# A two-layer propagation kernel: the index stages cut into pieces and run inside the sweeps beside them

## What is computed

```python
n, c, h, w = feature.shape
center = jnp.einsum('nchw,oc->nohw', feature, w_center)
step = jax.nn.relu(jnp.einsum('nchw,oc->nohw', feature, w_step))
prob = jax.nn.sigmoid(jnp.einsum('nchw,oc->nohw', feature, w_prob))
offset = jnp.transpose(center * step, (0, 2, 3, 1)) * STRIDE
th = jnp.minimum(jnp.round(gh[None] + offset[..., 0]), h - 1)
tw = jnp.minimum(jnp.round(gw[None] + offset[..., 1]), w - 1)
tgt = jnp.mod((th * w + tw).reshape(n, h * w).astype(jnp.int32), h * w)
sample = jax.vmap(lambda idx: grid_flat.at[idx].set(grid_flat))(tgt).reshape(n, h, w, 2)
...
sampled = _grid_sample_bilinear(feature, ngrid)
proped = sampled * prob + feature * (1.0 - prob)
return feature * prob + proped * (1.0 - prob)
```

## Time and profile before

| | us |
|---|---|
| median of 3 runs | 10036.8 (10035.82 to 10036.99) |
| the profiled execution | 10041.73 |
| its span | 10039.4 |
| busy: DVE, PE, POOL, ACT | 5791.8, 5688.7, 3805.1, 3314.3 |

### The profile page before, as it was taken

One profiled execution on the slowest core, in us unless ns is written; L12 is line 12 of the kernel. 1 busy time (PEld: TensorE's weight loads), 2 busy tenths in 40 slices (PEclk: granted clock), 3 DMA queues, 4 the chain that ended last, 5 costly groups with the idle time before them and its releaser, 6 DMA issues. The chain is left out here.

```text
span 10039.4 us, 85605 instructions
## 1 busy us (share of the span) xinstructions
PE 5688.7 (57%) x23732; PEld 2719.6 (27%) x23732; DVE 5791.8 (58%) x10809; ACT 3314.3 (33%) x6426; POOL 3805.1 (38%) x9006
## 2 busy tenths in 40 slices
PE   6841078311899988999700221888880011288888
PEld 2320033100444444444300110333330001133333
DVE  3347143571444434444389895666667989566666
ACT  5640066200444544445400000555450000054544
POOL 4530545204445544455400002666650000366665
PEclk8976589765889988899855665888895556588888
DMA  6851268513678876788710003666662000366665
GB/s 218 296 207 46 48 240 298 173 39 63 224 263 297 297 264 226 268 295 299 258 23 0 0 10 69 204 214 217 211 205 64 0 0 10 87 209 212 219 207 193
DMA packets 399395, 1675.31 MB, mean 167 GB/s; under 512 B 112501, under 2 KB 135772, under 8 KB 331621
## 3 DMA queue, kind: packets, MB, share of 16 engines
q1 hardware_dynamic: 203068, 908.43, 28.8%
q10 hardware_dynamic: 131400, 685.12, 16.8%
q0 software_dynamic: 64480, 76.57, 4.1%
HBM read 952.23 MB, written 727.72 MB: 167 GB/s over the span
## 5 line engine op out<-in xcount | busy, mean ns | idle before, releaser
L678 DVE TENSOR_TENSOR ps<-ps,arena 128x400 f32<-128x400 f32 x1600 | 929.9, 581 | 2088.6 <-PE ps L464 1161.7
L437 POOL DMA_INDIRECT arena<-table,gidx x1600 | 1616.5, 1010 | 954.6 <-issue 466.6
L457 PE MATMUL ps<-arena,minus 128*128 128x400 f32 x3200 | 1670.1, 606 | 396.0 <-DVE arena L680 260.2
L388 POOL TENSOR_TENSOR arena<-arena 128x32 f32<-128x32 f32 (+8 forms) x3450 | 808.3, 277 | 1876.2 <-issue 1066.1
L600 ACT ACTIVATE arena<-ps 128x400 f32<-128x400 f32 x1600 | 792.3, 495 | 2096.3 <-PE ps L451 1193.2
L487 PE MATMUL ps<-arena,w_conv 128*10 128x512 f32 (+1 forms) x2800 | 1205.9, 559 | 293.5 <-DMA arena<-x 283.7
L1173 POOL DMA_INDIRECT arena<-table,arena x160 | 151.9, 949 | 3137.4 <-DVEq L1208 2325.3
L606 ACT ACTIVATE arena<-iota,gcol 128x400 f32<-128x400 f32 x800 | 495.0, 619 | 2395.0 <-PEq L1208 2395.0
L540 ACT ACTIVATE arena<-ps 10x512 f32<-10x512 f32 (+1 forms) x1400 | 745.9, 540 | 1356.2 <-PE ps L487 1340.2
L500 PE MATMUL ps<-ident,arena 128*128 128x128 f32 x5000 | 844.8, 314 | 385.1 <-ACT arena L554 199.6
L1110 PE MATMUL ps<-ident,arena 128*1 128x128 f32 x4 | 1.5, 373 | 1731.3 <-DVE arena L856 1731.3
(11 more groups left out here) (195 smaller groups left out, 5357.3 us busy)
## 6 DMA issues: line engine op xcount, KB each, us to landing
arena<-x SPq DMA_DIRECT2D x200, 1600.0 KB
arena<-table SPq DMA_DIRECT2D x200, 1600.0 KB
table<-arena ACTq DMA_DIRECT2D x400, 512.0 KB, 2.7
y<-arena ACTq DMA_DIRECT2D x100, 1600.0 KB
arena<-y SPq DMA_DIRECT2D x100, 1600.0 KB
out<-arena ACTq DMA_DIRECT2D x100, 1600.0 KB
table<-arena ACTq DMA_DIRECT2D x200, 576.0 KB, 8.2
arena<-table,gidx POOLq DMA_INDIRECT x1600
```

The source lines that it names most:

```text
L388: last = E.tensor_tensor(tmp[:, :, at:at + size], cols[:, :, y + to:end + to:step], cols[:, :, y:end:step], ALU.subtract)
L437: pool.indirect_dma_start(got[:, m % DEPTH, e * C:(e + 1) * C], None, rows, bass.IndirectOffsetOnAxis(ap=gidx[:, 2 * m + e:2 * m + e + 1], ...
L457: nc.tensor.matmul(ps[:, 4 + r % 2, 0:W], minus[:, :], tile(t)[:, at], start=True, stop=False)
L678: V.tensor_tensor(d, d, g, ALU.mult).then_inc(s_mix, 1)
```

## The change

Every index stage runs inside a sweep: index 0 in sweep 1, index 1 in sweep 2, index 2 in sweep 3, index 3 in sweep 4. Sweeps 0 and 5 stay alone. The stage's engine functions are generators, and a sweep takes one piece of them per row (`next(work)`), on DVE, PE and ACT, and per tile or per group of four rows on POOL. A row of a sweep is called a slot here (8 a tile, 400 a sweep and some 16 behind). In sweep 1 DVE takes only 0.42 pieces a slot. What a loop with a runtime count holds is one piece: while it runs, DVE (and PE in the far loop) do nothing for the sweep.

```diff
-        sweep(0, None, 0)
-        alone_with(0)
-        sweep(1, None, 1)
-        alone_with(1)
-        sweep(2, 0, 2)
-        sweep(3, 1, 3)
-        alone_with(2)
-        sweep(4, 2, None)
-        alone_with(3)
-        sweep(5, 3, None)
+        sweep(0, None, 0, None)
+        sweep(1, None, 1, 0, pace=0.42, spell=99)
+        sweep(2, 0, 2, 1, spell=11)
+        sweep(3, 1, 3, 2, spell=3)
+        sweep(4, 2, None, 3)
+        sweep(5, 3, None, None)
...
+                def piece(ins, name=None):
+                    note(ins, name)
+                    yield
+                    dve.wait_ge(s_v, n[0])
...
+                compare(0)
+                for i in range(SIDE * SIDE):
+                    dve.wait_ge(s_v, loop0 + 2 * i + 1)
+                    if i + 1 < SIDE * SIDE:
+                        compare(i + 1)
+                    else:
+                        dve.wait_ge(s_v, n[0])
+                    note(V.tensor_tensor(near, near, hit[i % 2], ALU.max))
+                    yield
```

The index stage has its own memory (the first 22440 words of the arena) and PSUM banks 0 and 1. What the sweeps have left for themselves is smaller:

```diff
+            FR = 4 if tabling else 3
+            RR = 3 if listed else 2
+            GB = 2 if listed else 1
+            CB = 1 if mixing else 2
+            WB = 1 if mixing else 2
```

FR are tile buffers (were 4), RR buffers of half a tile of table rows (were two of a whole tile), GB and CB the PSUM banks of gate and products (were 2), WB the scratch of `blend_columns` (was 2). Products come in 8 chunks of 400 pixels instead of 7 of up to 512, and are stored in four pairs through two small buffers; a tile's three table stores go through two buffers instead of six:

```diff
                     def evacuate_conv(t, c):
-                        h = 0 if r < HALVES[0][1] else 1
-                        if r == a and t:
-                            act.wait_ge(s_cst[h], n * 16)
+                        count, nth = n * len(CHUNKS) + c, n * PAIRS + c // 2
+                        if c % 2 == 0 and nth >= 2:
+                            act.wait_ge(s_cst[nth % 2], nth // 2 * 16)
...
                     def evacuate(t, g):
-                        if g == a and t >= 2:
-                            act.wait_ge(s_tst[n % 2][q], n // 2 * 16)
+                        if g == a and nth >= 2:
+                            act.wait_ge(s_tst[nth % 2], nth // 2 * 16)
```

Rows that are blended go in batches of up to four, so that tiles 0 to 7 have two batches, the second of which waits on ACT for DVE's first. The far loop uses two PSUM banks: each of its 16 steps hands over four pieces of 400 columns instead of one of 1600. The index stage's DMAs were issued by SP and are now issued by ACT. Who blends a tile's columns is fixed when the program is made:

```diff
+            def owned(t):
+                if u_idx is None and not mixing:
+                    return "pool" if t % 2 else "dve"
+                now = (t + behind) * BROWS + 3
+                return "dve" if "moved" in born and now <= born["moved"] + BROWS * spell else "pool"
...
+                    if tabling:
+                        for t in range(TILES):
+                            if owner[t] == "pool":
+                                blend_columns(pool, nc.gpsimd, t)
+                            clock[0] = (t + behind + 2) * BROWS + 2
+                            next(work, None)
```

More of the change, by code:

```diff
@@ L93, with batches @@
 GROUPS = len(TURNED) * TILES + len(LATE)
-WEIGHED = [int(bool(INNER[t]) or t in LATE or t + 1 in LATE or t + 1 in EARLY) for t in range(TILES)]
-BLENDED = [int(bool(INNER[t]) or t in EARLY) for t in range(TILES)]
+def batches(t):
+    left, done = list(INNER[t]), []
+    while left:
+        closed = []
+        for y in left:
+            group, todo = {y}, [y]
+            while todo:
+                a = todo.pop()
+                for b in left:
+                    if FIX[b] == a and b not in group:
+                        group.add(b)
+                        todo.append(b)
+            closed.append(sorted(group))
+        best = min(closed, key=len)
+        if done and len(done[-1]) + len(best) <= NEARBY:
+            done[-1] += best
+        else:
+            assert len(best) <= NEARBY
+            done.append(list(best))
+        left = [y for y in left if y not in best]
+    carried = t in LATE or t + 1 in LATE or t + 1 in EARLY or t in EARLY
+    return done or ([[]] if carried else [])
+BATCHES = [batches(t) for t in range(TILES)]
+WEIGHED = [len(BATCHES[t]) if INNER[t] or t in LATE or t + 1 in LATE or t + 1 in EARLY else 0 for t in range(TILES)]
+BLENDED = [len(BATCHES[t]) if INNER[t] or t in EARLY else 0 for t in range(TILES)]
 def turned_before(u, t):
@@ new lines, in turn @@
+                    def turn(t, g):
+                        count, (j0, size) = turned_before(u_tab, t) + g, TURNED[g]
+                        if g == 0:
+                            blended(pe, t)
+                            if BLENDED[t]:
+                                pe.wait_ge(s_hb, counted(BLENDED, u_tab, t + 1))
+                        if count - u_tab * GROUPS >= 2:
+                            pe.wait_ge(s_tevac, count - 1)
+                        pixels = tile(t).rearrange("p (q k) -> p k q", k=COLS)
+                        for j in range(size):
+                            last = nc.tensor.transpose(ps[:, 2 + count % 2, j * PX:(j + 1) * PX], pixels[:, j0 + j, :], ident[:, :])
+                        last.then_inc(s_xpose, 1)
@@ new lines, in _ @@
+                    clock = [0]
+                    work = tensor(pe, clock)
+                    for t in range(ROUNDS):
+                        for r in range(BROWS):
+                            clock[0] = t * BROWS + r
+                            if mixing and here(t):
+                                row(t, r)
+                            elif r < PAIRS and tabling and here(t - behind):
+                                conv(t - behind, 2 * r)
+                            if r < PAIRS and tabling and here(t - behind):
+                                conv(t - behind, 2 * r + 1)
+                            if tabling and here(t - 2):
+                                for g in turns_at(r):
+                                    turn(t - 2, g)
+                            if r == BROWS - 1 and tabling and here(t - 2) and t - 2 in LATE:
+                                turn_late(t - 2)
+                            next(work, None)
@@ L1222, in _ @@
+                    clock[0] = 10 ** 9
+                    for _ in work:
                         pass
```

1537 lines of the change are left out of this document (775 added, 762 removed).

## The result

The changed kernel takes 9964.31 us (median of 8 runs, 9962.4 to 10010.59), the kernel before 10036.9 (8 runs). The ratio is 0.9929, with a 95% interval of 0.9916 to 0.9941: 0.7% faster, where 5.5% was forecast. The profiled execution took 9972.77 with a span of 9971.2.

What follows compares the result with a forecast made beforehand. PE idles in index stages (3618 us) and DVE bounds an ideal overlap; 19.6 + 858 + 1067 + 1850 + 2150 + 2209 + 1327 = 9481 us of span, said as 9480, 5.5% faster, range 8,800 to 9,880.

Steps and rivals of the forecast that it cites:

- DVE sets the pace of sweep 3: Sweep 3 with index 2: 3.9 us a slot set by DVE, 2150 us in sum for 2511 before.
- the store wait: Sweeps 0 to 3: ACT's products wait for a queued small store; 4.6 us a tile in sweep 0, 200 in sweep 2.
- The moved loops' hole: Sweep 2 behind tile 9: POOL's loops of 226 us delay tile 10's blend, while DVE and PE stand; 214 us.
- A far round: One round of the index stages' far loop, run inside a sweep: 82 us.
- The wait of ACT's third pair: Sweep 0: third product pair waits for the first pair's store, queued behind a table store; 4.5 us late a tile.
- Rival A: The store waits cost nothing, as small stores land early; about 8,870 us, chance 22 in 100.
- DVE's blends: Sweep 2, tiles whose columns DVE blends: the sum of 1850 us has no term for them.
- Index pieces in a PE-bound sweep: Sweep 2: DVE has room for most pieces, 30 us for the rest; sweep 1 with index 0 sums to 1067.
- Sweep 4: Sweep 4 with index 3: 310 slots at 5.15 us plus other terms, 2209 us for 2487.5 before.
- Rival B: POOL is shut out of memory while DVE runs index work; about 10,090 us, slower than before, chance 8 in 100.
- Rival C: PE's clock drops where DVE sets the pace, near 0.5 in sweep 3; about 9,840 us, chance 12 in 100.
- Half-tile loads "at nothing": Half-tile row loads cost nothing, as SP waits for buffers anyway; bounded by 1 us a tile, 50 a sweep.

Runs made afterwards that it cites:

- experiment 1: The changed kernel with four product buffers instead of two: 9037.02 us, ratio 0.900; on a further chip 8774.69 us.
- experiment 2: The changed kernel with POOL's moved loops one tile later in its program: 9680.77 us, ratio 0.9649.
- experiment 8: The changed kernel with four product buffers, POOL's loops one tile later and six table buffers in sweep 0: 8490.25 us, ratio 0.8441.
- experiments 1 and 4: The second: the changed kernel with four product buffers, POOL's loops one tile later and DVE blending all columns of sweeps 1 and 2: 9043.88 us.
- experiments 3 and 4: The first: the changed kernel with DVE blending all columns of sweeps 1 and 2: 9953.4 us, ratio 0.9922.

## Why the prediction was wrong

**Right.** Sweeps 3 and 4 gain most, and sweep 2 gains nothing from its overlap (though it was to come out even, and lost 390). DVE sets the pace of sweep 3 while it has pieces. The windows of the changed kernel, in sweep 3 and in sweep 4:

```profile
5000.00:5500.00 500.00, 381.91 (x1446) 165.39 (x1445) 473.65 (x485) 177.47 (x361) 388.30 (x700) 0.84 0.56 195
```

```profile
6800.00:8200.00 1400.00, 1045.28 (x3362) 429.81 (x3362) 1342.75 (x2209) 443.93 (x816) 988.28 (x551) 0.71 0.46 139
```

DVE is busy for 95 and 96% of them. That sweep 3 came out so near (2178 us for 2150) is luck in part: the store wait was put on every tile with pieces, at 3 us, and experiment 1 took 3 us in all from tiles 8 to 25, and 149 from the others. The moved loops' hole has the size, the place and the cause that were worked out (forecast 214, tile of 263 us; experiment 2: 191). A far round stays near 80 us: the tile with it in sweep 2 takes 115.3 between tiles of 33.7 and 41.2. The wait of ACT's third pair exists and costs 4.5 of idle time in sweep 0.

**The step that failed is the store wait: its size in the sweeps.** The prediction put it at 230, 22 x 4.6, 200 and 120, or 651 us. Experiment 1 took 899 out (254, 148, 345 and 152), so this term is 248 of the 490 us that are missing. Two parts of the working were short. In sweep 2 I took 5 us on 40 tiles. There the third pair waits 8.28, since the first pair's small store isn't done before the image store in front of it has landed: its issue to the end of the wait is 12.6 us. And in sweep 1 I counted the 22 tiles behind the index work alone. Besides, the sum took a wait for a loss of the same size, and with it PE's work grew (240 for 223 us in ten tiles of sweep 2). Rival A (the waits cost nothing, 8,870) was what such buffers would have given: with four the kernel takes 9037, or 8775.

The other 242 us are what experiment 1 leaves over my figures without store waits, 72 in sweep 0, 104 in sweep 1 and 244 in sweep 2, less 4 in sweep 3, and less the 155 and 18 by which sweeps 4 and 5 of the change came in below the forecast. In sweep 0 I had priced nothing but the wait: 30 of its 72 us lie in the first ten tiles, most of which have a second batch of blended rows, and experiment 8 took 31 away with table buffers. The prediction also gives sweep 0 one bank of products less; it has two, as before.

**DVE's blends were priced at nothing in sweep 2.** Tiles 11 to 21 of sweep 2 are DVE's; experiments 1 and 4 show 23 us a tile with POOL's blend and 30.7 with DVE's. In experiment 1 those ten tiles take 85 us more than in the kernel before.

**Index pieces in a PE-bound sweep cost more than DVE's free time suggests.** For sweeps 1 and 2 experiment 1 leaves 104 and 244 us over my figures without store waits. Of sweep 2's, by the distances of the tiles' first product stores in experiment 1 and in the kernel before: 85 are in the tiles with DVE's blends, 66 lie in the first eleven tiles (116 us more than before once far round and key loop are taken off; forecast 50), 46 are 1.7 us on each of the last 27 tiles, 19 are in the hole. The rest, and sweep 1's part, was not taken apart.

**Sweep 4 was 155 too dear.** 310 slots at 5.15 us carry the gaps of a sweep alone and of an index stage alone, and in the merged stage each fills the other's (96% busy above). DVE's two busy times, 842 + 978 = 1821, would have been the better start: it is busy 1748 of 2054.

**Rival B** (POOL shut out, slower): the stretch of POOL's operations is real, 286 to 655 ns in sweep 2, and POOL's gathers in sweep 4 (6800 to 8200) take 1800 ns, where those of sweep 5 take 1008. By the Trainium skill (SBUF — State Buffer, Who interferes with whom) a DVE operation with two inputs in SBUF contends with a GpSimd one that reads it; the hold for the whole instruction, with the other fully blocked, is what it says of the two-port modes. The trace agrees with the first in direction. DVE pays a little too: beside POOL's blends, in sweep 3, a maximum takes 1884 ns and a compare 1154, for 1819 and 989 in sweep 4. But in sweeps 3 and 4, where B had its price, DVE is busy for 95 and 96% of the time, so it doesn't wait for POOL; and in sweeps 1 and 2 experiments 3 and 4 took POOL's blends out and won nothing. **Rival C** (clock): the granted clock is 0.80 and 0.71 in sweeps 3 and 4, not near 0.5. In part it came in another place: where PE waits for a store, its clock is 0.87 for 0.99 (above).

**Half-tile loads "at nothing"** held where the result was measured (1308 us for 1327), but on three chips the changed last sweep takes 1073 to 1082 us, where the kernel before takes 1340 on one of them. That the half-tile loads are what makes it shorter isn't shown. The prediction's ground, that SP waits for buffers anyway, looked at who issues the load, and not at DVE, which in the kernel before waits 267.3 us there for it to land.

## What to carry to other kernels

Before two stages are overlapped, price what the sweep gives up for it by itself: here two product buffers cost 1377 us with no overlap at all, about as much as the overlap was worth (1347), and four fitted in partitions that nobody used. Here a small store behind a large one in the same queue counted as done only when the large one had landed, so a buffer that waits for it needs to last through the large one. Where an engine is the bound, a wait for something else can cost more than its length: PE's own work grew by 17 us in ten tiles beside 76 us of waits. And where a loop with a runtime count stands in one engine's program, look at what that engine owes the others right behind it: one position later was worth 191 us in sweep 2.

## What the runs showed of the hardware that I hadn't expected

The same kernel takes 9037 us on one chip and 8775 on another, and the change 9964 and 9683, with ranges of 50 us or less in each place, while the kernel before takes 10037 to 10062 at its median everywhere. The traces of the slower places have holes in the last sweep (in experiment 1, 63 of POOL's gathers start over 3 us behind the gather before, 255 us in all), those of the faster ones none. What makes them is open, and a cause that changed with the chip between the sets of runs isn't excluded.

A 31 KB store that was issued 2.9 us behind a 1600 KB one was not done for 12.6 us, and through 1100 us of steady tiles its buffer came free within 0.3 us of the large store's landing.

Pauses of PE cost more than their length: the same 971 matmuls took 240 us at a granted clock of 0.87, with waits between them, and 223 at 0.99 without. No run changed the clock alone.
